# Second attention of a decoder on one core: B products moved to GpSimd, causal mask moved into VectorE's maximum, input transposed earlier

## What is computed

```python
x = x + attn0(ln(x));  x = x + ssm0(ctx, ln(x));  x = x + ffn0(ln(x))   # ternary gate/up/down
x = x + attn1(ln(x));  x = x + ssm1(ctx, ln(x));  x = x + moe1(ln(x))   # 32 experts, 6 per token
# attn1: 16 query heads, 4 key/value heads, D = 128, S = 256
q, k = layernorm(q), layernorm(k);  q = q*cos + rot(q)*sin;  k = k*cos + rot(k)*sin
scores = q @ k.T / sqrt(128);  scores = where(causal, -inf, scores);  out = softmax(scores) @ v @ w_o
# ssm1: 256 channels, 16 states n; for each batch b and state n, over time t:
state[t] = state[t-1]*exp(delta[t]*A[n]) + delta[t]*u[t]*B[n,t];   y[t] += state[t]*C[n,t]
```

## Time and profile before

| | us |
|---|---|
| median of 3 runs (lowest to highest) | 911.28 (910.96 to 911.57) |
| the profiled execution's own time | 910.43 |
| its span in the profile | 908.6 |
| busy in the span: TensorE / VectorE / ScalarE / GpSimd | 755.5 / 680.0 / 490.2 / 353.0 |

### The profile page before, as it was taken

One profiled execution on the slowest core, in us unless ns is written; L12 is line 12 of the kernel. 1 busy time (PEld: TensorE's weight loads), 2 busy tenths in 40 slices (PEclk: granted clock), 3 DMA queues, 4 the chain that ended last, 5 costly groups with the idle time before them and its releaser, 6 DMA issues.

```text
span 908.6 us, 12577 instructions
## 1 busy us (share of the span) xinstructions
PE 755.5 (83%) x4080; PEld 582.3 (64%) x4080; DVE 680.0 (75%) x1102; ACT 490.2 (54%) x1062; POOL 353.0 (39%) x247
## 2 busy tenths in 40 slices
PE   6770579867898976699999999999955799999997
PEld 2240456544533554577877788878743689999996
DVE  4897689889758897788899898989967544444443
ACT  1743558640336602478777777688942354444442
POOL 1001356542341452133332333333533286666663
PEclk9785669998799997799999999999987899999999
DMA  4340223335020122011111111111400233443431
GB/s 171 121 170 26 70 113 120 116 117 220 0 76 0 61 57 92 1 36 43 51 35 48 47 36 47 48 37 50 159 2 1 96 142 139 139 139 141 139 136 46
DMA packets 28885, 74.65 MB, mean 82 GB/s; under 512 B 3632, under 2 KB 6336, under 8 KB 28448
## 3 DMA queue, kind: packets, MB, share of 16 engines
q1 hardware_dynamic: 28384, 71.51, 23.0%
q10 hardware_dynamic: 448, 2.49, 0.8%
HBM read 72.55 MB, written 1.44 MB: 81 GB/s over the span
## 4 chain that ended last, share of the span: by engine, by line
PE 57%; DVE 16%; issue 12%; ACT 11%; POOL 2%; DMA 1%; POOLq 0%; DVEq 0%; SPq 0%; ACTq 0%
PE ps L1857 6%; PE ps L1858 6%; PE ps L1859 6%; PE ps L1822 4%; PE ps L1698 4%; DVE hS L1030 4%; PE ps L1502 3%; PE ps L1792 3%; PE ps L1718 3%; PE ps L1810 3%; PE ps L1741 2%; PE ps L1742 2%; PE ps L1743 2%; DVE ps L1022 2%; PE ps L1791 1%
## 5 line engine op out<-in xcount | busy, mean ns | idle before, releaser
L420 POOL TENSOR_TENSOR hS<-hS,BCb 128x512 f32<-128x512 f32 x64 | 81.9, 1282 | 129.0 <-issue 71.0
L1454 DVE SCALAR_TENSOR_TENSOR arena<-ps,arena 128x1024 f32<-128x1024 f32 x32 | 39.2, 1225 | 102.0 <-ACT arena L896 93.1
L443 POOL TENSOR_TENSOR hS<-hS,BCb 128x1024 f32<-128x1024 f32 x23 | 56.1, 2439 | 108.0 <-DVE ps L1022 93.9
L506 POOL TENSOR_TENSOR MHl<-arena,MHh 128x1024 fp32r<-128x1024 f32 x34 | 81.8, 2405 | 16.7 <-ACT MHh L899 16.7
L1483 PE MATMUL ps<-ident,hS 128*128 128x128 f32 x256 | 41.2, 317 | 53.2 <-POOL hS L443 46.6
L1857 PE MATMUL ps<-Wh,MHh 128*128 128x256 f32 x272 | 77.8, 286 | 6.0 <-POOL MHl L506 6.0
L1060 DVE TENSOR_TENSOR_SCAN hS<-dA,ps 128x512 f32<-128x512 f32 x64 | 78.1, 1220 | 2.7 <-DVE ps L1051 0.6
L1858 PE MATMUL ps<-Wl,MHh 128*128 128x256 f32 x272 | 77.5, 285 | 0.0
L1859 PE MATMUL ps<-Wh,MHl 128*128 128x256 f32 x272 | 77.5, 285 | 0.0
L1483 PEld LDWEIGHTS ps<-ident,hS 128*128 128x128 f32 x256 | 34.0, 164 | 63.9 <-POOL hS L443 53.0
L503 POOL TENSOR_TENSOR Wl<-WB,Wh 128x512 fp32r<-128x512 f32 x34 | 47.2, 1389 | 64.2 <-ACT Wh L880 64.2
(11 more groups left out here) (243 smaller groups left out, 2107.6 us busy)
## 6 DMA issues: line engine op xcount, KB each, us to landing
BCb<-bc_dram SPq DMA_DIRECT2D x32, 512.0 KB, 3.6
BCb<-bcq_dram SPq DMA_DIRECT2D x64, 256.0 KB, 3.1
arena<-gate_dram SPq DMA_DIRECT2D x32, 512.0 KB, 3.7
WB<-in_we SPq DMA_DIRECT2D x34, 256.0 KB, 2.7
WB<-in_wqkv SPq DMA_DIRECT2D x1, 3072.0 KB, 12.9
WA<-in_wo ACTq DMA_DIRECT2D x1, 2048.0 KB, 7.8
WA<-in_ffn SPq DMA_DIRECT2D x1, 1408.0 KB, 7.3
pkb<-in_pk SPq DMA_DIRECT2D x2, 698.0 KB, 4.7
```

The costliest lines, as they stand in the source:

```text
L420: gp.tensor_tensor(h, h, qbc(q)[:, 1:2, :].broadcast_to([P, DT, S]), ALU.mult).then_inc(s["c_ready"], 1)
L443: gp.tensor_tensor(h, h, BCb[g % SB_LOADS][:, 1:2, :].broadcast_to([P, DT, HALF]), ALU.mult).then_inc(s["c_ready"], 1)
L506: gp.tensor_tensor(MHl[:, p, :], MH[p], MHh[:, p, :].bitcast(F32), ALU.subtract).then_inc(s["m_lo"], 1)
```

## The change

From step 10 on, the B products are made by GpSimd into the hS buffer, two steps ahead, and the scan works in place on SBUF; `times_cq` no longer waits for the next product there. The mask's matmul goes: VectorE's maximum becomes a `tensor_tensor_reduce` that writes minus scores minus mask back to PSUM and their minimum as bias, and the exponential takes a scale of -1. The low parts of the weights, the tables, `hidden_parts(0)` and the transposes of half 0 change places.

```diff
@@ gpsimd
+            def dbq(q):
+                b, n = q // DS, q % DS
+                pool.wait_ge(ld_bq[q % BRING], bq_count(q))
+                pool.wait_ge(s["du_ready"], 3 + b // 2)
+                pool.wait_ge(s["acc_mm"], LAYER_STEPS + q - HRING + 1)
+                gp.tensor_tensor(qring(hS, q), DU[:, :, batch(b)], qbc(q)[:, 0:1, :].broadcast_to([P, DT, S]),
+                                 ALU.mult).then_inc(s["dbu_ready"], 1)
             def times_cq(q):
                 pool.wait_ge(s["scan_done"], LAYER_STEPS + q + 1)
-                if q not in Q_GROUP_ENDS:
+                if q < Q_IN_FFN and q not in Q_GROUP_ENDS:
                     pool.wait_ge(s["dbu_ready"], LAYER_STEPS + q + 2)
...
             w1_low(0)
-            w1_low(1)
             for q in range(2):
                 times_cq(q)
+            w1_low(1)
+            for q in range(2, 5):
+                times_cq(q)
             w1_low(2)
-            for q in range(2, 8):
+            for q in range(5, 8):
                 times_cq(q)
             ln_rstd(3, (0,))
             for q in range(8, Q_IN_FFN):
                 times_cq(q)
+            ln_rstd(3, (1,))
+            pool.wait_ge(s["ln_h"], NT * 4)
+            dbq(Q_IN_FFN)
+            dbq(Q_IN_FFN + 1)
             w1_low(3)
-            w1_low(4)
-            ln_rstd(3, (1,))
-            w1_low(5)
...
             for kind, a in ATT1_PLAN:
                 if kind == "sum":
                     job(JOB[a])
-                elif kind == "dbu" and a > Q_IN_FFN:
-                    times_cq(a - 1)
+                    if JOB[a] < 2:
+                        w1_low(4 + JOB[a])
+                elif kind == "dbu":
+                    if a + 2 < QSTEPS:
+                        dbq(a + 2)
+                    if a > Q_IN_FFN:
+                        times_cq(a - 1)
@@ scalar: exp1, both activations
-                sc.activation(P1[p][:, 0:P], ps[:, 2 + p, 0:P], ACT.Exp, bias=nm1[:, p, 0:1],
+                sc.activation(P1[p][:, 0:P], ps[:, 2 + p, 0:P], ACT.Exp, scale=-1.0, bias=nm1[:, p, 0:1],
@@ vector
-                v.tensor_tensor_scan(f(qring(hS, q)), f(qring(dA, q)), ps[:, DBQ_BANK, :], 0.0, ALU.mult,
+                v.tensor_tensor_scan(f(qring(hS, q)), f(qring(dA, q)), ps[:, DBQ_BANK, :] if q < Q_IN_FFN else f(qring(hS, q)), 0.0, ALU.mult,
                                      ALU.add).then_inc(s["scan_done"], 1)
...
+                if j == PREP_DT:
+                    tables()
                 if j == PREP_DT + 1:
                     delta_round(2)
...
             ln_apply(3, 0)
-            tables()
+            hidden_parts(0)
             fd_residual(1)
             ln_stats(3, 1)
-            hidden_parts(0)
             ln_apply(3, 1)
...
             def max1(u):
                 p = u % 2
+                if u == 0:
+                    dve.wait_ge(ld["masks"], 48)
...
-                ch.step(v.tensor_reduce(nm1[:, p, 0:1], ps[:, 2 + p, 0:P], AX.X, ALU.max, negate=True))
-                v.tensor_reduce(nm1[:, p, 1:2], ps[:, 2 + p, P:3 * P], AX.X, ALU.max, negate=True).then_inc(s["s1_max"], 1)
+                for k, z in enumerate((slice(0, P), slice(P, 3 * P))):
+                    sc = ps[:, 2 + p, z]
+                    last = v.tensor_tensor_reduce(sc, sc, mask1[:, z], -1.0, 3.0e38, ALU.add, ALU.min, nm1[:, p, k:k + 1])
+                last.then_inc(s["s1_max"], 1)
...
-                elif kind == "dbu":
-                    dbq(a)
@@ tensor
             def fd(hf):
                 for t in range(4 * hf, 4 * hf + 4):
+                    if t == NT - 1:
+                        ln_tr(2, (0,))
...
-            ln_tr(2, (0,))
             ln_ready(2, 0)
...
-                diagonal = lambda z: z.rearrange("p (k n) -> p k n", k=3)[:, 0::2, :]
-                mm(diagonal(ps[:, 2 + p, 0:3 * P]), identb[:], diagonal(mask1[:]), start=True, stop=True, skip_group_check=True)
-                mm(ps[:, 2 + p, 0:P], q[:, h % REP1, 0:P], k[:, g, 0:P], start=False, stop=True, skip_group_check=True)
+                mm(ps[:, 2 + p, 0:P], q[:, h % REP1, 0:P], k[:, g, 0:P], start=True, stop=True, skip_group_check=True)
```

More of the change, by code:

```diff
@@ L827, in exp1 @@
                     act.wait_ge(s["pt1_mm"], u - 1)
-                sc.activation(P1[p][:, 0:P], ps[:, 2 + p, 0:P], ACT.Exp, bias=nm1[:, p, 0:1],
+                sc.activation(P1[p][:, 0:P], ps[:, 2 + p, 0:P], ACT.Exp, scale=-1.0, bias=nm1[:, p, 0:1],
                               accum_out=sum1[:, p, 0:1]).then_inc(s["s1_exp"], 1)
-                sc.activation(P1[p][:, P:3 * P], ps[:, 2 + p, P:3 * P], ACT.Exp, bias=nm1[:, p, 1:2],
+                sc.activation(P1[p][:, P:3 * P], ps[:, 2 + p, P:3 * P], ACT.Exp, scale=-1.0, bias=nm1[:, p, 1:2],
                               accum_out=sum1[:, p, 1:2]).then_inc(s["s1_exp"], 1)
```

## The result

The changed kernel takes 934.57 us (median of 4 runs, 933.34 to 937.71) against 911.12 us (4 runs, 910.02 to 911.57): ratio 1.0256, 95% interval 1.0237 to 1.0274. It is slower, by 23.4 us. The profiled execution took 934.87 us, its span is 933.1 (before 910.43 and 908.6).

What follows compares the result with a forecast made beforehand. TensorE was taken to set the pace, VectorE following closely with 30 us idle. Loop cycles +21, loop end +14 and lead-in -6 sum to +29 on 910.4, so 939.4; the median 0.9 above gives 940 us, range 904 to 960.

Steps and rivals of the forecast that it cites:

- The lead-in: Before the second attention's loop: reordered work starts the first rotation near 337 us (-9.5), 3.5 given back, net -6.
- B products to GpSimd: Second attention: 54 products take 39 us off VectorE and put 69 us onto GpSimd; taking work off has no direct price.
- The maxima: VectorE's masked maximum in the attention: 0.15 us more per unit, between 0 and 0.27; 10 us over 64 units.
- The mask's matmul: Attention scores: 0.11 us for each of 64 units, 7 us off TensorE, on the path only while TensorE sets it.
- The loop's cycles: Three-unit attention cycles go from 13.5 to 15.0 us by exclusion; 14 cycles, +21; four-unit cycles 0.
- The end of the loop: Last 14 scans, 32.8 us, each exclude two GpSimd products and take 46.7 us: +14, bounds +8 and +18.
- scalings are not broken up: Rival in the loop: VectorE keeps its turn through the eight scalings, cycle stays 13.5 us; 918 us, chance 0.15.
- Faster: Rival: the exclusion finds room where VectorE idles or reads PSUM, TensorE keeps the pace; 897 us, chance 0.19.
- The clock: Rival in the loop: stalls lower TensorE's granted clock from 0.98 to 0.90, +21; 961 us, chance 0.08.
- signs named beforehand: Changed profile: products near 1.6 us, scans and scalings stretched 1.1, cycle near 15, last 14 scans over 42, VectorE on chain.
- whole instructions: Loser of the SBUF lock blocks fully: seven handovers cost 1 us more per cycle, the sum some 14 us higher.
- small GpSimd reads cost nothing: Small GpSimd instructions beside VectorE: a root and a rope sum ran side by side at full speed.

Runs made afterwards that it cites:

- kernel 9: kernel 1 with the attention's 54 B products on VectorE cut to one column each, scans reading old contents; 903.09 us.
- kernel 3: The kernel before with only the causal mask moved into VectorE's maximum; 910.1 us, ratio 0.9979 to before.
- Kernel 2: The kernel before with only the B products on GpSimd and the scan in place; 938.7 us, ratio 1.0289 to before.
- kernel 6: Changed kernel with GpSimd's order alone changed: product pair ahead of the root, products after the rope wait for the eight scalings; 915.53 us.
- kernel 5: Changed kernel with attention scans reading the PSUM bank's old contents, GpSimd still making its products and scans waiting for them; 929.03 us.
- the parts alone: Three runs on the kernel before, each with one part: B products on GpSimd, mask in maximum, lead-in order; 938.7, 910.1, 905.5 us.
- kernel 1: Changed kernel with the B products and their PSUM bank back on VectorE and the C product's wait back; 904.07 us.
- kernel 7: Changed kernel with kernel 6's GpSimd order and the last 14 B products (steps 50 to 63) back on VectorE in PSUM; 902.23 us.

## Why the prediction was right

It said 940 us (924 to 957 for the likeliest case), and it was 934.6. Its mechanism holds, and its two largest terms were too large: the cycles by 1.9 us, the end of the loop by 3.6. The lead-in's -6 came out as -5.8 with some luck, out of two terms that were each some 2 us off.

- **B products to GpSimd.** The text said that work off VectorE has no direct price, and kernel 9 shows it for all 54 products (with the mask and the lead-in as changed). The price was in the exclusion, as said.
- **The maxima.** I took 0.15 us more per unit, between 0 and 0.27. The rows of the changed kernel:

```profile
550.72 0.13 DVE L1384 RECIPROCAL rc<-sum 128x2 f32<-128x2 f32 x1
550.77 0.27 DVE L1376 CUSTOM_DVE_ANT_0 ps<-ps,mask 128x128 f32<-128x128 f32 x1
550.97 0.14 DVE L1376 DVE_READ_ACCUMULATOR2_ANT nm<- 128x1 f32 x1
550.97 0.46 DVE L1376 CUSTOM_DVE_ANT_0 ps<-ps,mask 128x256 f32<-128x256 f32 x1
551.35 1.22 DVE L1341 TENSOR_TENSOR arena<-ps,tabs 128x1024 f32<-128x1024 f32 x1
```

  From rc to rotation 0.63 us, and 0.59 before (544.29 to 544.88): +0.04. In the two other units of this cycle it is 0.65 and 0.72 to the next instruction, and 0.59 and 0.62 before: +0.2 us for the three, less than half of the 0.45 that I took. 128 columns take 0.27 from an SBUF mask and PSUM; the read of the accumulator (0.14) runs beside the next instruction.
- **The mask's matmul.** 7 us of TensorE, "on the path only while TensorE sets it". TensorE leads the chain in kernel 3 and still only 1.7 us came; 1.5 us turned into waits like the one shown, and the rest is open. Longer maxima could be part of it, which was not tried.
- **The loop's cycles.** Predicted 15.0, measured 14.96; +21 for 14 of them, measured +18.1 for thirteen and +1.0 for the four-unit cycles, which I had at 0. The details were less good than the sum, and that the cycle fits to 0.04 us is in part luck. I had three GpSimd instructions going between the scalings. There are two, one ahead of the first and one behind it, since the C product ran ahead of the rope sum: VectorE had waited 0.78 us for ScalarE (rc at 557.45), which my count did not have, and the rope sum asked 0.08 us behind the C product. The scalings ended 9.73 us behind the row sum (564.62 less 554.89), predicted 9.45. Kernel 2 shows the case that I had counted: its rope sum is issued at 563.55, 0.01 us ahead of the C product, and takes 1.21; the C product takes 2.34, and the eight scalings 5.15.
- **The end of the loop.** Predicted +14 (8 to 18) with the last 14 scans over 46.7 us; they took 39.5 (646.84 to 686.34), +6.7 and below the lower bound, and the end as a whole grew by 10.4. The term that was too large is 46.7 us for "each now excludes two GpSimd products". Where both engines are busy without a gap this is what happens:

```profile
670.60 2.27 DVE L1077 TENSOR_TENSOR_SCAN hS<-dA,hS 128x512 f32<-128x512 f32 x1 [0.19 <-POOL hS L419]
673.96 2.28 DVE L1077 TENSOR_TENSOR_SCAN hS<-dA,hS 128x512 f32<-128x512 f32 x1 [1.10 <-POOL hS L419]
```

```profile
670.53 1.26 POOL L429 TENSOR_TENSOR hS<-hS,BCb 128x512 f32<-128x512 f32 x1
671.75 2.18 POOL L419 TENSOR_TENSOR hS<-DU,BCb 128x512 f32<-128x512 f32 x1
```

  The scan waits for the C product, the B product for the scan, and a step takes 3.36 us (3.6 predicted). But the 14 scans met fewer products than the 25 that I had counted. From scan 50 to 684.00 only ten B and ten C products are issued: four B products had been made before, and the last four C products run from 684.00 on. Another 2.5 us lie ahead of scan 50 (14.8 us behind the last rotation, before 12.35), in the last job's rope sum and scalings. The last rows show the rest:

```profile
684.07 2.27 DVE L1077 TENSOR_TENSOR_SCAN hS<-dA,hS 128x512 f32<-128x512 f32 x1 [1.09 <-POOL hS L419]
694.31 0.69 DVE L1404 TENSOR_TENSOR X<-X,ps 128x512 f32<-128x512 f32 x1 [7.91 <-PE ps L1841]
```

```profile
684.00 5.86 POOL L429 TENSOR_TENSOR hS<-hS,BCb 128x512 f32<-128x512 f32 x4
```

  The last scan ends at 686.34, but its C product is the fourth of a row that ends at 689.86, since GpSimd runs behind with C products; before, it ended 1.4 us behind the scan.
- **The lead-in.** First rotation predicted near 337 (-9.5), measured 334.94 (-11.6); given back up to job 3 predicted 3.5, measured 5.8; net -6, measured -5.8. W1's low parts in the scalings were priced at 3.5 us for both. They cost about 4, and one shows in the chain:

```profile
334.94 1.23 DVE L1341 TENSOR_TENSOR arena<-ps,tabs 128x1024 f32<-128x1024 f32 x1
...
342.57 4.15 DVE L1364 SCALAR_TENSOR_TENSOR arena<-arena,jst,tabs 128x128 f32<-128x128 f32 x8
...
353.19 4.18 DVE L1364 SCALAR_TENSOR_TENSOR arena<-arena,jst,tabs 128x128 f32<-128x128 f32 x8 [1.89 <-POOL jst L502]
```

```profile
353.47 1.99 issue
```

  Eight scalings take 4.15 and 4.18 us instead of 2.19. In the second group the 1.99 us that the chain calls "issue" are the wait behind the first scaling for a GpSimd w1_low.
- **The sum**: +21 + 14 - 6 = +29 predicted; +19.1 + 10.4 - 5.8 + 0.7 = +24.4 measured. By the whole instructions of the Trainium skill ("SBUF — State Buffer", section "SBUF: two separate sides") it would have been some 14 us more; the rows' handovers were the better price (cycle 14.96 us, 15.0 by the rows, 16.0 by whole instructions).

Of the rivals, "scalings are not broken up" is refuted by their 4.14 us, and its 918 is what kernel 6 comes near to by keeping GpSimd away from them. "Faster" assumed that the products find VectorE idle or at PSUM; kernel 6 shows this for the cycles alone, and for an order made for it (13.46 us), not for this one. The clock did not fall (0.98). And all 54 scans read SBUF (hS<-dA,hS). Of the signs named beforehand, products near 1.6 us (1799 and 1426), a cycle near 15, VectorE on the chain and scalings in stretched times came; the scans are stretched at the end of the loop (1815 ns) and not in the cycle shown (1.22 us), where the rope sum is; "last 14 scans over 42 us" did not come.

What stays open: the 1.7 us behind the last scan in kernel 5, and 4.6 us between the sum of the parts alone (+18.8) and the whole (+23.4) by medians. The traces don't show these 4.6 us: up to the last residual the three parts alone give +29.9, -0.6 and -5.1, together +24.2, and the whole +23.8. Kernel 2's profiled execution took 941.05 us, 2.35 above its median. Within the traces the shares shift. The B part alone adds 16.8 us to the loop (237.9 to 254.7) and 11.9 to its end, on top of kernel 1 it adds 21.8 (235.3 to 257.1) and 10.8, since with the B products on GpSimd the cycle is about as long with the mask's matmul as without (14.82 and 14.96). The 0.14 us can be found: in kernel 2 the maxima have no mask, and from rc to the instruction behind them the three units of a cycle take 0.57, 0.59 and 0.62 us, against 0.64, 0.65 and 0.72 in the changed kernel, where VectorE sets the pace.

## What to carry to other kernels

Before work is moved off an engine, take it away altogether in one run: here 54 products on VectorE weighed 1 us at most, so no other place for them could have gained more than that. Where two engines exclude each other, count each instruction's place and not its number: the same 54 B products on GpSimd cost 30.5 us (changed kernel) or 11.5 (kernel 6) over kernel 1, by what they stood beside. A run of many short instructions was the worst neighbour for a run of long ones here (1.95 us lost by eight scalings, 1.05 by one rope sum), because the turn can go over at each of them, while reads of PSUM and the row sum were good ones. The best version here (902 us, kernel 7) is no better than the simple one that leaves the products where they were (904, kernel 1).

## What the runs showed of the hardware

Three things that I had not expected. A small GpSimd instruction that asks first costs VectorE nothing: a root of 8 columns (L502, 555.26, 1.64 us) and a scan with two SBUF inputs (L1077, 555.46, 1.22 us) run side by side, though both read two tiles of SBUF. When it asks second it is held like a large one. In kernel 6 it asked once 0.03 us behind a scan and took 2.62 us:

```profile
615.02 1.22 DVE L1084 TENSOR_TENSOR_SCAN hS<-dA,hS 128x512 f32<-128x512 f32 x1
```

```profile
615.05 2.62 POOL L502 TENSOR_TENSOR jst<-jst,mhalf 128x8 f32<-128x8 f32 x1
```

So the prediction's "small GpSimd reads cost nothing" holds for VectorE, and not for the root itself. Which of the two goes first is decided within 0.1 us: with 0.08 us between the requests the rope sum lost 1.05 us, and 0.01 us ahead of the C product it lost nothing (kernel 2, 563.55). And a masked maximum, add and minimum over 128 or 256 columns with the mask in SBUF, costs 286 and 464 ns where the plain reduction takes 279 and 415, and its accumulator's read next to nothing.
